# Attention scores on TensorE: in each half quarter the order transposed, plain, plain, transposed

## The reference

```python
x = x + _layernorm(_L0_attn_ref(_layernorm(x), q_w, k_w, v_w, out_w, out_b))   # x: (16, 512, 128)
# 16 heads of 8, blocks of 64 keys; for each block:
scores = einsum('bhqd,bhkd->bhqk', Q, K_blk) * SCALE
m_new = maximum(m, scores.max(-1))
corr = exp(m - m_new)
exp_scores = exp(scores - m_new)
l_new = chunk_sum * corr + chunk_sum
out_new = out * corr + einsum('bhqk,bhkd->bhqd', exp_scores, V_blk)
# at the end: out / l
```

## Time and profile before

| | |
|---|---|
| median of 3 runs | 1793.39 us (1789.89 to 1798.41) |
| profiled execution | 1789.92 us, its span 1788.0 us |
| mean granted TensorE clock | 0.941 of full speed |
| PE / weight loads busy | 1583.6 / 874.2 us |
| DVE / ACT / POOL busy | 1328.3 / 1147.1 / 712.2 us |
| score matmuls run | from 37.4 to 858 us |
| steady loop of this stage | about 190 to 740 us |

### The profile page before, as it was taken

How to read it: one execution, slowest core, us unless ns; L and a number is a source line. 1 busy time by engine, 2 the same in 40 slices (tenths; PEclk the granted TensorE clock), 3 DMA queues, 4 the chain that set the end, 5 groups by cost and what they waited for, 6 DMA issues and landing times. The chain is left out here.

```text
span 1788.0 us, 35516 instructions
## 1 busy us (share of the span) xinstructions
PE 1583.6 (89%) x8576; PEld 874.2 (49%) x8577; DVE 1328.3 (74%) x3585; ACT 1147.1 (64%) x2294; POOL 712.2 (40%) x1011
## 2 busy tenths in 40 slices
PE   4999999999999999999499999999498973899996
PEld 2333333333333333333277777777345542566664
DVE  5899999999999999997256666666357763466664
ACT  1587888888888888888366666666236553343342
POOL 2224343434444434222413333333135776244444
PEclk7799999999999999999699999999799985899998
DMA  5333223323222233210100000000120113222210
GB/s 129 82 90 100 85 81 95 90 72 94 84 83 85 82 88 85 84 54 22 45 32 1 1 0 0 0 0 1 32 68 18 46 47 107 62 59 61 57 55 17
DMA packets 84447, 102.50 MB, mean 57 GB/s; under 512 B 15995, under 2 KB 49537, under 8 KB 84368
## 3 DMA queue, kind: packets, MB, share of 16 engines
q1 hardware_dynamic: 78992, 88.89, 17.9%
q0 software_dynamic: 5376, 12.66, 2.1%
HBM read 61.44 MB, written 35.33 MB: 54 GB/s over the span
## 5 line engine op out<-in xcount | busy, mean ns | idle before, releaser
L836 DVE TENSOR_REDUCE bmax<-PS 128x8 f32<-128x512 f32 x1024 | 651.5, 683 | 53.7 <-PE PS L577 51.1
L689 ACT ACTIVATE EX<-PS 128x512 f32<-128x512 f32 x1024 | 565.2, 604 | 106.2 <-PE PS L588 96.5
L577 PE MATMUL PS<-KR,QR 33*128 33x512 f32 x1024 | 411.0, 469 | 43.2 <-DVE bmax L836 30.9
L588 PE MATMUL PS<-QR,KR 64*128 64x512 f32 x1024 | 399.0, 460 | 1.6 <-ACT EX L689 1.5
L577 PEld LDWEIGHTS PS<-KR,QR 33*128 33x128 f32 x1024 | 166.9, 188 | 358.8 <-DVE bmax L836 298.3
L598 PE MATMUL PS<-EX,VS 128*9 128x512 f32 x2048 | 267.9, 595 | 1.2 <-ACT EX L689 1.2
L588 PEld LDWEIGHTS PS<-QR,KR 64*128 64x128 f32 x1024 | 162.4, 185 | 11.3 <-ACT EX L689 10.2
L1035 PE MATMUL PS<-pA,wb 128*128 128x512 f32 x640 | 157.4, 402 | 0.0
L774 POOL TENSOR_TENSOR m_diff<-m_prev,m_all 128x16 f32<-128x16 f32 x64 | 14.2, 223 | 326.9 <-DVE m_all L848 326.9
L1864 ACT ACTIVATE g<-PS 128x512 f32<-128x512 f32 x72 | 43.0, 597 | 142.9 <-PE PS L1824 142.9
L1035 PEld LDWEIGHTS PS<-pA,wb 128*128 128x128 f32 x640 | 120.7, 192 | 27.5
(11 more groups left out here) (227 smaller groups left out, 2829.7 us busy)
## 6 DMA issues: line engine op xcount, KB each, us to landing
QR<-q_scr SPq DMA_DIRECT2D x256, 64.0 KB, 2.4
KR<-k_scr SPq DMA_DIRECT2D x256, 64.0 KB, 2.3
k_scr<-partsB SPq DMA_DIRECT2D x42, 256.0 KB, 2.9
rows<-row_scr SPq DMA_DIRECT2D x72, 129.0 KB, 2.1
q_scr<-partsB SPq DMA_DIRECT2D x28, 256.0 KB, 3.0
X<-in_L_attn_x SPq DMA_DIRECT2D x16, 256.0 KB, 3.0
X<-x SPq DMA_DIRECT2D x16, 256.0 KB, 2.4
xB<-in_L_attn_x SPq DMA_DIRECT2D x14, 256.0 KB, 3.3
```

Source lines behind the costliest of these rows:

```text
L577: pe.matmul(PS[:, bank_of(i, n), :], QR[rows, i, h // 2, t * P:(t + 1) * P], KR[rows, i, h // 2, :], start=True, stop=True).then_inc(tile_ ...
L588: pe.matmul(PS[:, RING3 + bank_of(j, n), :], KR[rows, j, h // 2, kt * P:(kt + 1) * P], QR[rows, j, h // 2, :], start=True, stop=True).then ...
L689: act.activation(EX[:, n % (2 * HG), :], PS[:, RING3 + bank_of(j, n), :], ACT.Exp, scale=SCALE).then_inc(ex_set, 1)
L836: dve.tensor_reduce(bmax[:, i % 2, n, :], PS[:, bank_of(i, n), :].rearrange("p (b k) -> p b k", k=BLK), AX_X, ALU.max).then_inc(tile_max, 1)
```

## The change

One string in PE's program: in each half quarter the first two scores change places. The third and the fourth, the value matmuls and everything else stay.

```diff
@@ -655,7 +655,7 @@
-                ORDER = "sTsTvsTsT"
+                ORDER = "TssTvTssT"
 
                 def step(b, i, g, has):
                     for q in range(NT):
```

## The result

The changed kernel takes 1795.44 us (median of 20 runs, 1791.61 to 1801.27), the kernel before in the same comparison 1790.54 us (1784.46 to 1798.41): ratio 1.0032, 95% interval 1.0021 to 1.0043. It is a little slower, within the half per cent that the forecast called no change, but the interval leaves 1 out. So there is a loss of some 4 to 8 us to explain, where the prediction's sum had +0.6. Single runs of one kernel spread over some 10 to 14 us, so the ratio alone can't say where such a loss comes from.

What follows compares the result with a forecast made beforehand. PE and DVE were taken to pace each other, ACT having some 15% of room. Profiled 1789.92 us plus 0.6 for swaps, 0 for group starts and pairs gave 1790.5, or 1794.0 shifted to the three-run median; range 1786 to 1801.

Steps and rivals of the forecast that it cites:

- the rival of strict alternation: Score matmuls alternating row halves free the third load, 0.11 us at each of 121 DVE waits: 13.3 us, 1780.1; chance 0.06.
- A pair of groups as long as now: Steady stretch: sign of a right forecast, that two groups together take the same time as before the change.
- The even group starts: 31 first halves: transposed load 0.23 us earlier, plain 0.11 later; bounds -7.1 and +3.4 us, both taken as 0.
- The carried gain: Rival at even group starts: earlier transposed scores carry through exponentials and value matmuls, -7.1 us, 1786.3; chance 0.06.
- the held plain score: Rival at even group starts: transposed score waits for ACT and holds the plain one, 10.5 us slower, 1803.9; chance 0.06.
- idle time before transposed loads well above 0.1 us: Weight-load track: sign that the forecast is wrong and the plain score is held behind ACT.
- The swaps themselves: 496 swaps of each half's first two scores: 0 to 1.2 us lost at DVE's 121 waits, +0.6 us taken.
- it doesn't do what it says: Rival: the array takes each row half's work in its own turn, so order counts for nothing; 1793.4 us, chance 0.06.

Runs made afterwards that it cites:

- The series: Separate kernel, nine series: full-array matmuls, then plain and transposed matmuls in their own row groups, with or without reports; plain end to DVE start 37 to 125 ns.
- the halves exchanged: New order with row halves exchanged between plain and transposed scores, each head getting its neighbour's maxima, against the kernel before: ratio 1.0020.
- The control: The kernel before, unchanged, run once more beside itself like an experiment: ratio 0.9991 (0.9981 to 1.0000).
- the loop alone: New order only in groups 12 and later, against the kernel before, run twice: ratios 1.0006 and 1.0019.
- the even starts only: New order only in the first half of the even groups, against the kernel before: ratio 0.9991 (0.9982 to 1.0000).

## Why the prediction was right, and its one wrong term

The forecast of no measurable change held: 1795.44 us against 1794.0, inside its own 1786 to 1801, and within 0.5% of before. How near the two times are is luck: 1794.0 was built on the median of three runs, 1793.39, and the 20 runs of the kernel before have 1790.54. Measured from there the change cost 4.9 us, not 0.6. Its steps:

- Both first matmuls still start in the same hundredth, the third load comes 0.11 behind, a pair still takes 0.24. Right, and with it the rival of strict alternation falls. "A pair of groups as long as now" was wrong by 0.10 of 24.94 us.
- The even group starts. The transposed load was to come 0.23 earlier and the plain one 0.11 later, with nothing reaching DVE. It is 0.24 earlier and 0.07 later in group 30, DVE's first reduction is unmoved, and this part of the change alone leaves the turn at 49.88. The carried gain and the held plain score fall with it, although a transposed score does wait for ACT once a turn. The sign that was named for it, idle time before transposed loads well above 0.1 us, was badly chosen: it came (180.6), and nearly all of it was idle time that had been booked on the plain loads.
- **The swaps themselves: mis-sized.** The step "exchanging two instructions that start in the same hundredth of a microsecond moves each by less than 0.01 us", which gave 121 x 0.01 = 1.2 us at most and +0.6 in the sum, reckoned with starts. Starts move by 0.003. What moves by 0.031 is the time at which DVE learns of the end. With 80 waits in 500 us of the kernel before, 8 a turn, that is 0.25 us a turn; measured are 0.20 in the first profiles and 0.22 in the mean of all three of the changed kernel and two of the kernel before. No run shows why it isn't all of the 0.25. Over 62 groups, 15.5 turns, 0.20 to 0.22 make 3.1 to 3.4 us, 0.17 to 0.19%. ACT, which now hears 0.03 us earlier, gave nothing back: that gain was rightly put at nothing. The upper bound of 1.2 was wrong too: it was drawn from the precision of the printed starts, and a bound has to hold for the whole way from one engine to the next.
- The rival "it doesn't do what it says" falls: the order of two matmuls that run side by side does count, by the order of their reports.

The kernel before showed this already. In its half at 403.28 both matmuls end at 403.77 or 403.78, DVE starts 0.04 later and ACT 0.07. I had read the row of DVE and not that of ACT beside it. The Trainium skill also has the rule: TensorE: Matmul & The Clock Gate, Part 3 (The cost: per-tile semaphore tail), says that reports of tiles that finish together are made one after the other, and fits 26.3 ns for each report and 4.7 ns for each tile. The series agree: 29 to 34 ns for a report with its matmul, 14 ns for three silent matmuls.

What stays open in part is the rest of the measured difference. The loop's lengthening gives a ratio of 1.0018; the whole change was measured at 1.0032, 1.0034 and 1.0015, and with the halves exchanged at 1.0020. The control's 0.9991 shows that such ratios scatter by 0.001, and the low clock at the start lasts 37.5 to 58 us with no order that these few profiles show. The estimates at equal clock go some way: 4.6, 3.8 and 3.5 us for the whole order, 2.1 and 2.5 for the loop alone (11 turns, 2.2 to 2.4 expected), and -0.2 for the control. So part of the second ratio, 1.0034 or 6.1 us, goes with the clock, which differs from run to run. What is left beyond the loop's 3.1 to 3.4 us is 0.1 to 1.5, about as much as these estimates are uncertain; that it is chance is likely but not shown. No version that was run beats the kernel before: the even starts only, at 0.9991, come out like the unchanged control.

## What to carry to other kernels

When matmuls run side by side in different row groups, their ends coincide but their reports queue: put first the one for which the pacing engine waits. In a wait that repeats hundreds of times read the whole way in the timeline, from the producer's end to the consumer's start and for each of the consumers, since 0.03 us can hide between two rows whose starts look alike. And where a few tenths of a per cent matter, take the length of one turn of a steady loop: it told 0.08 us of 50 apart in single profiles (profiles of one kernel agree within 0.02), where ratios of whole runs, from 8 to 20 runs of the changed kernel each, still scattered by 0.001 and more.

## What the runs showed of the hardware

- A finished matmul's report holds the next one's back by 0.03 us: 38 ns from end to waiting engine for the first, 68 to 72 for the second, 125 for the fourth. A matmul without a report costs those behind it about 5 ns (14 for three).
- The granted clock at the start of the attention rose from 1.2 to 2.4 GHz after anything from 37.5 to 58 us of low clock, and in some executions fell again for 3.4 to 13.6 us in all; the same program gave 37.5 and 44.4 + 6.8 us. Ahead of the fall at 134.3 us in the changed kernel's first profile PE was busy for 2.90 of 4.00 us (130 to 134), where the kernel before, which stayed at 2.4 GHz there, had 4.00 of 4.00. The first reduction of group 16 came between 243.26 and 253.90 us in these profiles, of which the new order makes up at most 0.9; that scatter is three times the effect that was looked for.
- Behind the loop the profiles scatter as much: from the first reduction of group 52 to the end of the span they take 1092.5 to 1101.7 us, the kernel before itself 1095.8 and 1093.3. The stages behind the attention are the same program in all of them.
